# Ffn of two tiles at a time by seven block products, attention bias as a value row, exponentials head by head with sums by ACT: a gated cross-attention and ffn layer on one Trainium2 core

## The reference, cut to what matters

```python
# x: (4, 2048, 512), ctx: (4, 77, 384), 16 heads of 64, all float32
x = x + tanh(g_xattn) * attention(layernorm(x), ctx, Wq, Wk, Wv, Wo, bo)
x = x + tanh(g_ffn) * (layernorm(x) @ W[idx] + b[idx])       # W[idx]: 512 x 512
# attention: q = xn @ Wq, k = ctx @ Wk, v = ctx @ Wv, softmax(q k / 8) v per head, @ Wo + bo
# idx = argmax(log_softmax(logits) - log(-log(u))), one of eight ffn weights
```

## Time and profile before

| what | value |
|---|---|
| median of 3 runs | 1081.31 us (1080.05 to 1082.87) |
| the profiled execution, its own time | 1080.38 us |
| its span | 1078.4 us |
| granted TensorE clock, mean | 0.997 of full speed |
| PE, DVE, ACT, POOL busy | 98%, 88%, 32%, 28% of the span |

### The profile page before, as it was taken

How to read it: one execution, slowest core, us unless ns; L and a number is a source line. 1 busy time by engine, 2 the same in 40 slices (tenths; PEclk the granted TensorE clock), 3 DMA queues, 4 the chain that set the end, 5 groups by cost and what they waited for, 6 DMA issues and landing times.

```text
span 1078.4 us, 16498 instructions
## 1 busy us (share of the span) xinstructions
PE 1053.7 (98%) x5497; PEld 531.7 (49%) x5497; DVE 946.7 (88%) x1447; ACT 349.5 (32%) x599; POOL 305.9 (28%) x445
## 2 busy tenths in 40 slices
PE   8978999999999999999999999999999999999998
PEld 6633454445444554445544554445544455445443
DVE  3787989989999999999999999999999999999995
ACT  3555522323223232323223232232323232232331
POOL 0555442222212222222212222122222222122221
PEclk9999999999999999999999999999999999999999
DMA  8502455454545555454545545454554545455543
GB/s 310 107 2 69 79 118 111 110 118 106 126 98 121 109 115 115 104 124 105 121 105 114 116 108 125 98 122 107 117 113 106 122 105 123 104 115 115 111 98 93
DMA packets 332923, 120.87 MB, mean 112 GB/s; under 512 B 311984, under 2 KB 313060, under 8 KB 332900
## 3 DMA queue, kind: packets, MB, share of 16 engines
q1 hardware_dynamic: 332836, 120.57, 50.1%
q0 software_dynamic: 64, 0.00, 0.0%
HBM read 26.16 MB, written 16.78 MB: 40 GB/s over the span
## 4 chain that ended last, share of the span: by engine, by line
PE 93%; DVE 3%; DMA 2%; issue 1%; ACT 1%; SPq 0%; POOL 0%; DVEq 0%
PE banks L1061 85%; PE banks L1260 3%; PE banks L1164 1%; PE banks L1100 1%; PE banks L1091 1%; DMA late<-late 1%; PE banks L1172 1%; PE banks L1153 1%; DVE vw_area L848 1%; DMA fold_area<-in_L_xattn_Wv 1%; ACT vw_area L660 0%; DVE late L864 0%; DMA early<-early 0%; DMA early<-late 0%; PE banks L1278 0%
## 5 line engine op out<-in xcount | busy, mean ns | idle before, releaser
L1061 PE MATMUL banks<-fold_area,early 128*128 128x462 f16 (+1 forms) x2304 | 412.3, 337 | 3.2 <-issue 2.8
L1061 PE MATMUL banks<-vw_area,late 128*128 128x512 f16 x1701 | 377.4, 379 | 2.7 <-DMA late<-late 1.6
L1061 PEld LDWEIGHTS banks<-fold_area,early 128*128 128x128 f16 x2304 | 224.3, 97 | 192.1 <-issue 5.3
L1061 PEld LDWEIGHTS banks<-vw_area,late 128*128 128x128 f16 x1701 | 166.2, 98 | 193.6 <-DMA late<-late 2.0
L572 POOL TENSOR_TENSOR stats<-stats,cst 128x1 f32<-128x1 f32 x64 | 12.1, 189 | 655.4 <-DVE stats L1003 655.4
L938 DVE TENSOR_REDUCE stats<-banks 128x6 f32<-128x462 f32 (+1 forms) x192 | 111.6, 581 | 72.5 <-PE banks L1061 72.5
L1061 PE MATMUL banks<-late,last_slot 128*128 128x512 f16 x744 | 170.7, 379 | 0.0
L699 ACT ACTIVATE late<-last_slot 128x512 f16<-128x512 f32 x64 | 40.3, 630 | 316.0 <-DVE last_slot L1015 316.0
L734 ACT ACTIVATE late<-late,cst 128x462 f32<-128x462 f32 (+1 forms) x192 | 120.6, 628 | 58.7 <-DVE late L944 58.7
L749 ACT ACTIVATE late<-late 128x1024 f16<-128x1024 f32 (+1 forms) x66 | 69.0, 1046 | 207.8 <-DVE late L957 207.8
L1061 PEld LDWEIGHTS banks<-late,last_slot 128*128 128x128 f16 x744 | 72.4, 97 | 88.2
(11 more groups left out here) (114 smaller groups left out, 717.2 us busy)
## 6 DMA issues: line engine op xcount, KB each, us to landing
early<-in_x SPq DMA_DIRECT2D x64, 256.0 KB, 2.7
out<-last_slot SPq DMA_DIRECT2D x64, 256.0 KB, 2.3
fold_area<-in_L_xattn_Wo SPq DMA_DIRECT2D x4, 512.0 KB, 10.2
fold_area<-in_L_xattn_Wq SPq DMA_DIRECT2D x2, 1024.0 KB, 11.9
fold_area<-in_L_xattn_Wk SPq DMA_DIRECT2D x2, 768.0 KB, 12.5
late<-late SPq DMA_TRANSPOSE x66, 4.9
last_slot<-in_L_ffn_W SPq DMA_DIRECT2D x1, 1024.0 KB, 8.1
early<-early SPq DMA_TRANSPOSE x64, 3.1
```

The source lines that it names most:

```text
L1061: mm = nc.tensor.matmul(ps, lhs(l), rhs(r), start=first and n == 0, stop=last and n == 2)
```

## The change

Seven things change together.

- **Ffn.** Two tiles (256 rows) are taken together and their 256 x 512 by 512 x 512 product is made as a product of two-by-two blocks by seven block products (Strassen's form with shared sums) instead of eight. `PAIRS` is 30, so the first 60 tiles go in pairs; the last four go alone (`lone`, 30 matmuls of 256 columns each). A product is 6 matmuls of 256 columns. Products 0 and 1 stand behind the scores of an even step, 2 and 3 behind its attention; 4 and 5 behind the scores of the odd step, 6 behind its attention. Three half banks (`chain`, `side_sum`, `cross`) take them, and DVE adds seven parts of 256 columns to the residual (`added`).
- **Operand sums.** POOL makes four sums of 256 columns for each pair. Instead of one transposed operand of 512 columns for each tile there are three and a half for a pair, each with a high part on ACT, a low part on DVE and a transpose on SP's queue.
- **Weights.** The ffn weight is loaded a second time behind the folding, POOL makes sums of its quarters, and ACT and DVE split seven quarters.
- **Exponentials.** ACT reads the scores from PSUM, one head (77 columns) an instruction, with the negated scaled maximum as bias, and has the sum accumulated (`accum_out`). The shifts, and the sums on DVE, are gone; a small product for each bank (the maxima by minus the scale) is new. A bank is free when its exponentials are done: four banks in a ring (`s_bank`) in place of six.
- **Probabilities** are scaled, rounded and split in two pieces (12 heads, 4 heads) in each step, not only in the first and the last.
- **Bias.** `bo` is a row of the value matrix, against a constant column of the probabilities, so POOL's residual is gone; the residual stays in the ring `xr` of eight tiles that x was loaded into, and is stored from there. The store of two tiles and the load of two others that need their place stand at the head of each even step on SP's queue.
- **Folding order.** `VISITS` starts with three projections, the query turns are shared between ACT and DVE, and a fifth value is staged.

The diff, cut to its core:

```diff
+    def exponentials(o, m, k):
+        h0, h1 = BANKS[k]
+        act.wait_ge(nmx_ready, nth(o, m, len(BANKS)) + k + 1)
+        for h in range(h0, h1):
+            nc.scalar.activation(probs[:, h * J:(h + 1) * J], s_bank(m, k)[:, (h - h0) * J:(h - h0 + 1) * J], ACT.Exp,
+                                 bias=nmx[:, h:h + 1], scale=exp_scale, accum_out=sums[:, h:h + 1]).then_inc(exp_done, 1)
-    nc.scalar.activation(probs[:, cols], probs[:, cols], ACT.Exp, scale=exp_scale).then_inc(exp_done, 1)
...
+    def maxima(o, m, k):
+        nc.vector.reduce_max(mx[:, h0:h1], by_head(s_bank(m, k)), AX.X).then_inc(mx_ready, 1)
+        dve.wait_ge(mx_ready, nth(o, m, NB) + k + 1)
+        nc.vector.tensor_scalar(nmx[:, h0:h1], mx[:, h0:h1], nexp_scale, None, ALU.mult).then_inc(nmx_ready, 1)
-    def shift(k):
-        nc.vector.tensor_tensor(by_head(probs[...]), by_head(s_ps[b % 2][...]), mx[...].to_broadcast(...), ALU.subtract).then_inc(shifted, 1)
...
-    nc.vector.reduce_sum(sums[:, h0:h1], values, AX.X).then_inc(sum_ready, 1)
...
+    def product(o, m, i):
+        place = (chain, side_sum, chain, cross, chain, cross, chain)[i]
+        for k in range(2):
+            mm = split_products(place, lambda s: x2[:, s, k, :], lambda s: wf_split[:, i, s, k, :], start and k == 0, k == 1, i in (2, 4, 5, 6))
+        mm.then_inc(f_done, 1)
-    for k in range(KT):
-        mm = split_products(place, lambda s: turned[:, s, k, :], lambda s: wf_split[:, s, k, :], k == 0, k == KT - 1)
...
+    # SP, head of an even step
+    sp.wait_ge(f_added, nth_pair(*ended, PRODUCTS) + PRODUCTS)
+    for tile_done in (ended, ended_next):
+        sp.dma_start(out[batch, rows, :], xr[:, tile_done[1], :]).then_inc(out_stored[tile_done[1]], 16)
+    for lag in (2, 3):
+        load_x(ol, ml)          # waits for out_stored of that place
+    due(x2_lo, nth_pair(*pair, GROUPS) + 3)
+    turn_group(2)
```

More of the change, by code:

```diff
@@ L131, in flamingo_layer @@
+        wf_sum = [room.rearrange("p (k n) -> p k n", k=2) for room in (xr[:, RING - 2, :], xr[:, RING - 1, :], room_b)]
+        c = Carve(work)
+        c.at = folds
         kT = c.take(HP * BJ).rearrange("p (h n) -> p h n", h=HP)
         wqT = c.take(HP * D).rearrange("p (h n) -> p h n", h=HP)
[L133 to L137, removed]
@@ L236, in is_first, with tile, valid, nth @@
[L236 to L242, removed]
+        def tile(o, m, lag):
+            return o + (m + lag) // RING, (m + lag) % RING
+        def valid(o):
+            return not isinstance(o, int) or 0 <= o < NT // RING
+        def nth(o, m, per=1):
+            return o * (RING * per) + m * per
+        def nth_pair(o, m, per=1):
+            return o * (RING // 2 * per) + m // 2 * per
@@ new lines, in step @@
+            def step(o, m):
+                even = m % 2 == 0
+                o1, m1 = tile(o, m, 1)
+                op, mp = tile(o, m, -1)
+                o2, m2 = tile(o, m, -2)
+                ended = tile(o, m, -6)
+                pair = tile(o, m, -4 if even else -3)
+                begun = tile(o, m, -4 if even else -5)
+                grouped = valid(pair[0]) and paired(*pair)
+                multiplied = valid(begun[0]) and paired(*begun)
+                ahead = valid(o1) and not is_tile(o, m, 0)
+                if valid(o2):
+                    dve.wait_ge(x2_stats, nth(o2, m2) + 1)
+                if even and valid(ended[0]) and paired(*ended):
+                    added(*ended, 6)
+                if not even and multiplied:
+                    added(*begun, 2)
+                    added(*begun, 3)
@@ L1044, in step @@
-                if is_last(q, b):
-                    output()
-                if is_last(q2, b2):
-                    output(*tile(q, b, -4))
-                if valid(q3) and not valid(q) and not near_last(q3, b3, 2):
-                    output()
-                if valid(qp) and not (valid(q) and between):
-                    attention_sum()
+                if grouped:
+                    group_low_of(*pair, 2 if even else 0)
+                if not even and is_tile(*pair, 2 * PAIRS):
+                    lone_low(2 * PAIRS)
@@ new lines, in step @@
+            def step(o, m):
+                even = m % 2 == 0
+                op, mp = tile(o, m, -1)
+                begun = tile(o, m, -4 if even else -5)
+                multiplied = valid(begun[0]) and paired(*begun)
+                if valid(o):
+                    scores(o, m)
+                if multiplied:
+                    product(*begun, 0 if even else 4)
+                    product(*begun, 1 if even else 5)
+                if is_tile(o, m, NT):
+                    lone(2 * PAIRS)
+                if valid(op):
+                    attention(op, mp)
+                if multiplied and even:
+                    product(*begun, 2)
+                    product(*begun, 3)
+                if multiplied and not even:
+                    product(*begun, 6)
+                if is_tile(o, m, NT):
+                    lone(2 * PAIRS + 1)
+                    lone(NT - 2)
+                if is_tile(o, m, NT + 1):
+                    lone(NT - 1)
```

988 lines of the change are left out of this document (584 added, 404 removed).

## The result

| what | before | after |
|---|---|---|
| median | 1082.09 us (4 runs, 1080.05 to 1084.99) | 1131.06 us (4 runs, 1129.76 to 1131.98) |
| ratio of after to before | | 1.045, 95% interval 1.0422 to 1.0477 |
| span of the profiled execution | 1078.4 us | 1129.0 us |

What follows compares the result with a forecast made beforehand. The prediction took PE's matmuls to bound each step, before and after (15.11 to 14.82 us). Its terms, -17.7 + 2.8 + 2 + 2 = -10.9 us, gave a span of 1067.5 and a time of 1070.5 us, range 1060 to 1096.

Steps and rivals of the forecast that it cites:

- PE's term: Ffn on PE: 109.4 ns a matmul of 256 columns, step 14.82 us for 15.11, -17.7 us over 60 tiles.
- The rival of weight loads: PE's ffn: weight loads not hidden under 256 columns, up to 0.46 us a step and 1097 us; chance 0.08.
- DVE's sum: DVE's work in a step: 3.6 us removed, 2.9 added, 13.1 us of 14.82, so it fits.
- The round through ACT: Chain from one step's maxima to the next's: mean 8.5 + 14e, 14.5 us, inside PE's step; as bound, chance 0.22.
- e: One head's exponential on ACT: between 0.35 and 0.58 us, taken as 0.43; below 0.45 the chain stays under PE's step.
- SP's queue: Even steps: third group's transpose behind stores and loads, within 0.5 us of need; rival that it is late, chance 0.13.
- Its own rule: SP's queue: 1.0 us late every other step makes the mean chain 15.0 us, the time 1081; 0.3 us late, nothing.
- so I cost this at nothing: Probabilities' transposes: land some 2 us ahead of their attention, no cost; without that cover each 0.1 us is 6 us.
- The folding: Before the first scores: stays 98.95 us, value scale's later load against better spread over ACT and DVE, plus or minus 4.
- Start and end: First four steps: +2 us from DVE's weight split; end: +2 us; four lone tiles on PE: +2.8 us.
- the last pair's gain: PE's saving behind tile 62: 0.6 us of the 60 tiles' 17.7 us.

Runs made afterwards that it cites:

- run 14: Kernel of run 13 with a hint at the top of the loop's body announcing the branch back: 1074.43 us, ratio 0.9937.
- run 5: Changed kernel with the bias load early, the loop written out and the loads of x behind the transposes: 1080.97 us, ratio 1.0007.
- run 10: Kernel of run 6 with exponentials head by head but no accumulated sum, DVE summing in two pieces: 1094.54 us, ratio 1.0124.
- run 13: Changed kernel, loop kept: bias load early, loads of x behind transposes, ffn bias later, last variance and normalization ahead of tile 61's output: 1088.27 us.
- run 11: Control: the kernel before the change with its loop of four tiles written out: 1085.89 us, ratio 1.0049.
- run 1: Changed kernel with only the load of bo moved ahead, behind the loads of ctx: 1119.98 us, ratio 1.0352.
- run 6: Kernel of run 5, with ffn bias scaled behind the third tile's exponentials and last variance ahead of tile 61's output: 1077.02 us, ratio 0.997.

## Why the prediction was wrong, point by point

**PE's term was right.** 12 matmuls of 256 columns take 507.53 - 506.22 = 1.31 us, 109.2 ns each against 109.4. A weight load is at 98 ns a row and shows nowhere. Once nothing else held PE, 58 steps took 860.4 us (859.0 in run 14) against 859.6 forecast, and an eighth product cost 18.9 us (30 x 0.656 = 19.7). The rival of weight loads is excluded by the same rows.

**DVE's sum was right.** 12.9 us against 13.1.

**The round through ACT did not bound.** e is 0.39 us, forecast 0.43, limit 0.45; the read-out costs 0.09. In runs 5 and 14 the chain with the same heads runs at PE's pace. By the prices of the Trainium skill ("ScalarE: Activation LUTs", What ACT_TABLE_LOAD costs) a head without the read-out is 0.343 us, an estimate; the trace of run 10 has 0.305, so the measurement decides.

**The step that failed: SP's queue, "By my sums it arrives within 0.5 us of need", with no term in the sum for it.** The third group arrived 1.38 us late in the step shown, 35.6 us in 30 even steps, about 1.2 each, and moving the loads gave back 23.5 us. The prediction names the wait for the stores, with 2.3 us to landing; how it came to 0.5 us is not shown. What its text gives no time for is SP's own issuing: in the step shown the rows of the two stores and of the two loads are 0.87 and 0.96 us long, the wait between them is 1.40 (40.6 us over 37 waits in the list of SP's waits), and the transpose stands 3.50 us behind the first store. The rival was the right mechanism, too small in size, and given a chance of 0.13. Its own rule (1.0 us late makes the mean chain 15.0) with the 1.2 us measured gives 14.5 + 0.6 = 15.1 us a step and some 16 us; 23.5 came back, so by this rule the chain without the late group was a little over 14.5 too, though it stayed under PE's step, as run 14 shows. The late group turned the whole gain of PE into waiting, as the eighth product at no cost shows. The transposes of the probabilities, of which the prediction says "so I cost this at nothing", were rightly costed: PE never waits for them in the changed kernel's loop.

**A step that was missing: the jump of the loop.** The body grew from four steps to eight and nothing in the prediction asked what that costs. Writing the loop out gave back 12.2 us, the hint 13.8 between runs 13 and 14. The page of before had the fact that bears on it: 9 instruction transfers over twelve jumps, against 78 over six after. The Trainium skill ("Runtime: NRT & Kernel Launch", Instruction fetch mechanics) says that a taken branch to code outside the pages held stalls for the fetch of its target. The trace agrees with this rule. The page says that kernels prefer full unrolling where possible for this reason; run 11 measures the opposite for the kernel before, 0.5% slower.

**The clock, for which the sum had no term.** Behind three of the six jumps of the changed kernel the next step is 16.2 us long in place of 14.48. Its scores, and the granted clock (the third number from the right), show why:

```profile
345.60 8.11 PE L1288 MATMUL banks<-fold_area,work 128*128 128x462 f16 x36 [2.64 <-DMA work<-work]
```

```profile
345.70:349.10 3.40, 3.40 (x10) 1.34 (x10) 3.05 (x8) 0.63 (x1) 0.11 (x1) 0.50 0.66 124
```

PE had waited 2.64 us; then the clock stood at 1.2 GHz for 3.4 us, and 36 matmuls took 8.11 us in place of 6.43. Three times 1.7 us are 5.1. At the other three jumps PE waited as long (2.5 to 2.8 us), at run 13's six 1.6 to 2.3, and the clock did not fall; what decides it stays open.

**The folding, "98.95 us stays my estimate, plus or minus 4".** It was 12.8 us later. The prediction named the cause, the value scale behind a load, and let it cancel against a better spread folding, within 4 us. The load lands at 31.46 us, DVE waits 12.0 us for it, PE 10.95 us behind DVE, and the granted clock is 0.51 from 28 to 42 us: the 24 matmuls behind the wait take 8.98 us, in run 1 6.39. 11.1 us came back in run 1.

**Start and end, +2 and +4.8 together with the lone tiles.** They were +5.9 and +7.8 (the forecast's +4.8 meets the last pair's gain of 0.6 there, so 4.2 in the table). At the start DVE's 4.70 us for seven quarters (run 6) delays the next x. The clock takes a part too: in the changed kernel PE waits 5.21 and 5.27 us in this stage, and behind these waits 27 matmuls of the attention take 7.40 us in place of 5.99 and 36 of the scores 8.25 in place of 6.43; the granted clock of the stage is 0.92, against 0.97 before. At the end 1.9 us (55.2 to 53.3) were the order on DVE, the last variance and normalization behind an output that waits for PE. These are why even the best version is at 1074 and not 1070. Of the 17.7 us gained in the middle, run 14's profiled execution, the slowest of its six, gives back 9.0 up to tile 4 (4.4 of them before the first scores, a time that scattered from 99.5 to 103.4 us over the kernels with the early bias load) and 5.9 behind tile 62.

So the change's main terms held, and three things beside them, 50 us together, undid it: a wait in a queue, a load, and a jump. The other 10 us to the forecast (run 5) are the start and the end.

## What to carry to other kernels

A saving on the busiest engine is real only if the rounds around it have the same slack: test it by giving the engine its old work back, and if that costs nothing, look for the wait. In an in-order queue cost every wait and every issue, the queue's wait for its own stores too, for everything behind it. And when a loop's body grows, compare the count of instruction transfers before and after, and hint or shorten the loop.

## What was not expected of the hardware

- The accumulated sum costs 0.09 us a head although its row lasts 0.21 us on the mean: the next ACTIVATE starts 0.09 us behind the read-out's start.
- A jump back over eight steps' code left DVE idle for 3.1 us and stretched a step by 2.0 us on the average in run 13 (17.13 against 15.14), by up to 3.0 in the changed kernel; a hint at the body's head took it away, and 78 instruction transfers became 17.
- The same program written out is not free either: 5 us slower for the kernel before, though PE had bounded every step. A dozen transposes came late, for a reason not found.
- A wait of PE can cost more than its own length: behind one of 2.64 us the clock was at 1.2 GHz for 3.4 us, 1.7 us more; behind others of the same kind it was not.
